# Attention and a routed feed-forward layer on one core: four payload buffers, the last group's scatters set among the tiles, and the words of all tiles loaded from SyncE's queue

## What is computed

```python
x = x + xattn(ctx, ctx, layernorm(x), Wk, Wv, bv, Wq, bq, Wo, bo)
xt = layernorm(x).reshape(-1, D)                       # 4096 tokens
p = softmax(xt @ Wr + br); probs, idx = top_k(p, 2); probs /= probs.sum()
h = layernorm(relu(xt @ W1[e] + b1[e])) * g1[e] + be1[e]
y = layernorm(relu(h @ W2[e] + b2[e])) * g2[e] + be2[e]
x = x + sum over the token's two experts of gate * y
```

## Time and profile before

| what | value |
| --- | --- |
| time, median of 3 runs | 272.37 us (269.18 to 274.11) |
| profiled execution, from first to last instruction | 268.4 us |
| between the two, taken as what lies around the span | 4.0 us |
| TensorE busy | 239.9 us (89%) |
| VectorE busy | 229.7 us (86%) |
| ScalarE busy | 211.5 us (79%) |
| GpSimd busy | 190.6 us (71%) |
| mean granted TensorE clock | 0.955 |

### The profile page before, as it was taken

How to read it: one execution, slowest core, us unless ns; L and a number is a source line. 1 busy time by engine, 2 the same in 40 slices (tenths; PEclk the granted TensorE clock), 3 DMA queues, 4 the chain that set the end, 5 groups by cost and what they waited for, 6 DMA issues and landing times.

```text
span 268.4 us, 10286 instructions
## 1 busy us (share of the span) xinstructions
PE 239.9 (89%) x2960; PEld 194.0 (72%) x2960; DVE 229.7 (86%) x1091; ACT 211.5 (79%) x795; POOL 190.6 (71%) x300
## 2 busy tenths in 40 slices
PE   1989779899888677679899999999999999999994
PEld 1564567777666434579899979999999999999330
DVE  0667986867689989689999988999999999999875
ACT  2465675789888888757999988999999999999700
POOL 8602277877757777775888888888888888878640
PEclk9997995899999759999999999999999999999999
DMA  6998398123425234354333443333315686772257
GB/s 159 313 299 295 91 271 279 51 89 92 139 82 136 83 91 99 84 119 94 84 90 67 89 82 81 73 72 75 84 33 142 155 155 141 149 143 86 68 187 233
DMA packets 48676, 34.56 MB, mean 129 GB/s; under 512 B 26871, under 2 KB 42743, under 8 KB 48620
## 3 DMA queue, kind: packets, MB, share of 16 engines
q1 hardware_dynamic: 38972, 22.80, 32.8%
q0 software_dynamic: 6592, 9.00, 12.7%
q10 hardware_dynamic: 3056, 2.11, 2.6%
HBM read 15.11 MB, written 12.02 MB: 101 GB/s over the span
## 4 chain that ended last, share of the span: by engine, by line
DVE 37%; issue 22%; PE 20%; ACT 9%; DMA 5%; DVEq 4%; SPq 1%; ACTq 0%
PE bank L721 15%; DVE vo L1873 8%; PE bank L725 4%; DMA w2f<-in_L_ffn_W 3%; DVE rs L1914 3%; DVE cx L1903 3%; DVE kq L1866 3%; DVE w2f L1653 3%; DVEq L1880 2%; DVE st L1891 2%; ACT ex L1175 2%; DVE mv L1897 1%; DMA wr<-in_L_ffn_Wr 1%; ACT xt L1198 1%; DVE topi L1573 1%
## 5 line engine op out<-in xcount | busy, mean ns | idle before, releaser
L679 POOL DMA_INDIRECT answers<-vo,words_of x71 | 70.6, 994 | 23.8 <-issue 19.4
L667 POOL DMA_INDIRECT slot_rows<-pay,pos x64 | 65.5, 1023 | 27.9 <-issue 18.5
L721 PE MATMUL bank<-kb_room,w1h 128*128 128x128 f16 x568 | 55.2, 219 | 1.7 <-issue 1.7
L725 PE MATMUL bank<-w2h,rh 128*128 x284 | 51.4, 219 | 1.6 <-ACT w2l L1122 1.6
L725 PE MATMUL bank<-rh 128*128 128x129 f16 x284 | 51.5, 220 | 0.0
L725 PE MATMUL bank<-w2l,rh 128*128 x284 | 51.4, 219 | 0.0
L721 PE MATMUL bank<-kb_room,w1l 128*128 128x128 f16 x284 | 51.2, 219 | 0.0
L1866 DVE SCALAR_TENSOR_TENSOR kq<-bank,rh 128x512 f16<-128x512 f32 x71 | 47.8, 673 | 0.1
L721 PEld LDWEIGHTS bank<-kb_room,w1h 128*128 x568 | 43.6, 98 | 2.6 <-issue 2.6
L1347 ACT ACTIVATE rh<-bank 128x512 f16<-128x512 f32 x71 | 41.1, 579 | 5.2 <-PE bank L721 4.2
L705 POOL DMA_DIRECT2D words_of<-slot_rows x71 | 40.8, 576 | 2.0 <-issue 1.8
(11 more groups left out here) (259 smaller groups left out, 601.7 us busy)
## 6 DMA issues: line engine op xcount, KB each, us to landing
x_tok<-in_x SPq DMA_DIRECT2D x8, 256.0 KB, 7.7
w1f<-in_L_ffn_W SPq DMA_DIRECT2D x2, 1024.0 KB, 8.8
pay<-pay SPq DMA_DIRECT2D x8, 256.0 KB, 3.3
w1f<-answers SPq DMA_DIRECT2D x8, 256.0 KB
w2f<-answers SPq DMA_DIRECT2D x8, 256.0 KB, 2.9
kb_room<-slot_rows SPq DMA_TRANSPOSE x71, 3.3
words_of<-slot_rows POOLq DMA_DIRECT2D x71, 1.0 KB
answers<-vo,words_of POOLq DMA_INDIRECT x71
```

The source lines that it names most:

```text
L667: eng.indirect_dma_start(slot_words, bass.IndirectOffsetOnAxis(ap=pos[:, g % 2, k, i:i + 1], axis=0), pay[g % 2][:, k, i, :].bitcast(U32), ...
L679: eng.indirect_dma_start(answers, bass.IndirectOffsetOnAxis(ap=words_of[:, j % NW, 0:1], axis=0), z[j % NZ], None).then_inc(s_ans[j % NZ], 16)
L721: return eng.matmul(dst, lhsT, rhs, start=start, stop=stop)
L725: return eng.matmul(dst, lhsT, rhs, start=start, stop=False, skip_group_check=True)
```

## The change

- `pay`, `pos` and the semaphores `s_copy` and `s_sc` are four (NP = 4) where they were two; group g waits for the scatters of group g - 4.
- All 8 scatters of the last group are issued among the tiles, at p = 0, 2, ..., 14.
- `words` moves from GpSimd to SyncE. `words(j)` is issued right behind the transposing load of tile j + 8 (`WORDS_BEHIND`), and the last eight behind the last tile's load. It takes the row number from the register that the load of tile j used. It waits for the answers of tile j - 12 and for `gate_share(j - 8)`.
- GpSimd has neither the word loads nor the register loads for them.
- Smaller edits free room and semaphores: `b2row` and `w2_rows` lie in rows of `w2_mean` and `c2`, the load of `b2row` goes ahead of W1's, several semaphores are joined, and some waits are merged with their neighbours.

```diff
+    NP = 4
-        b2row = sb("b2row", [1, E * D])
-        w2_rows = sb("w2_rows", [2, E * D])
         c2 = sb("c2", [P, E * D])
+        b2row, w2_rows = w2_mean[0:1, :], c2[0:2, :]
-        pay = [sb(f"pay{n}", [P, K, GT, ROW], F16) for n in range(2)]
+        pay = [sb(f"pay{n}", [P, K, GT, ROW], F16) for n in range(NP)]
-        NW, NS, LEAD = 12, 8, 2
+        NW, NS = 12, 8
+        WORDS_BEHIND = E
@@ sync
+            def words(j):
+
+                if j >= NW:
+                    eng.wait_ge(s_ans[(j - NW) % NZ], answered(j - NW))
+                if j >= NS:
+                    eng.wait_ge(s_rg, j - NS + 1)
+                eng.dma_start(words_of[:, j % NW, :], slot_words[bass.ds(place_of[j], P), D:]).then_inc(s_word[j % NS], 16)
...
                     for j in range(NX):
                         tile_rows(j)
+                        if j >= WORDS_BEHIND:
+                            words(j - WORDS_BEHIND)
...
                 tile_rows(j)
+                words(j - WORDS_BEHIND)
 
                 if j in back_at:
                     answers_back(back_at[j])
 
+            for j in range(SLOT_TILES - WORDS_BEHIND, SLOT_TILES):
+                words(j)
@@ gpsimd
-            for g in range(GROUPS):
+            for g in range(GROUPS - 1):
                 for k in range(K):
                     for i in range(GT):
-                        if g < GROUPS - 1 or k == 0:
-                            payload_out(g, k, i)
+                        payload_out(g, k, i)
+            last_out = [(GROUPS - 1, k, i) for k in range(K) for i in range(GT)]
...
-            for j in range(LEAD):
-                words(j)
             for p in range(SLOT_TILES + 4):
                 if 0 <= p - 4 < SLOT_TILES:
                     answer(p - 4)
-                if p + LEAD < SLOT_TILES:
-                    words(p + LEAD)
-
-                if p % 3 == 2 and p // 3 < GT:
-                    payload_out(GROUPS - 1, 1, p // 3)
+                if p % 2 == 0 and p // 2 < K * GT:
+                    payload_out(*last_out[p // 2])
@@ scalar (and likewise in pos_ and gate_rows)
-                if g >= 2:
-                    eng.wait_ge(s_sc[g % 2], scattered(g - 2))
+                if g >= NP:
+                    eng.wait_ge(s_sc[g % NP], scattered(g - NP))
```

More of the change, by code:

```diff
@@ L388, in build @@
                 "rstd2_guess", "xt", "pay_hi", "pay_lo", "mask", "pe_rank", "pos", "pe_base"))
-        s_copy = [signal(f"pay_copy{n}") for n in range(2)]
-        s_sc = [signal(f"scatter{n}") for n in range(2)]
+        s_copy = [signal(f"pay_copy{n}") for n in range(NP)]
+        s_sc = [signal(f"scatter{n}") for n in range(NP)]
         q_stat, q_root1, q_root2, q_max, q_sum, q_top, q_pos, q_scale, q_tab, q_gate = (signal(n) for n in (
@@ L395, in build @@
         s_diff, s_gexp, s_gated, s_gate = (signal(n) for n in ("gate_diff", "gate_exp", "gates_in_rows", "gates"))
[L397 to L402, removed]
+        s_share, p_share, s_shareT, p_off = (signal(n) for n in (
+            "shares", "pe_shares", "sharesT", "pe_offsets"))
+        s_gm, s_ss, p_tot, s_tot, s_scale, s_w1x = (signal(n) for n in (
+            "gains", "square_sums", "pe_totals", "totals", "scale", "w1_less_last"))
         p_rows, s_rows_, st_sums, ld_off, s_c2, p_low, s_low = (signal(n) for n in (
@@ L428, in scattered, with rows_out @@
         def scattered(n):
-            return 16 * K * GT * (n // 2 + 1)
+            return 16 * K * GT * (n // NP + 1)
+        def rows_out(eng, groups):
+            for g in range(max(groups - NP, 0), groups):
+                eng.wait_ge(s_sc[g % NP], scattered(g))
         def answered(j):
@@ L483, in sync @@
             eng.dma_start(gb[NB:2 * NB, :], flat("L0_ffn_be1").rearrange("(c p) -> c p", p=P)).then_inc(ld_gb, 16)
+            eng.dma_start(b2row[:, :], flat("L0_ffn_b2").rearrange("(o n) -> o n", o=1)).then_inc(ld_gb, 16)
             for h in range(2):
@@ L489, in sync @@
                                   ).then_inc(ld_w1[h], 16)
-            eng.dma_start(b2row[:, :], flat("L0_ffn_b2").rearrange("(o n) -> o n", o=1)).then_inc(ld_b2, 16)
-            eng.wait_ge(s_diag, 1)
+            eng.wait_ge(s_zeros, 1)
             for n in range(2):
@@ L510, in sync @@
             regs = [eng.alloc_register(f"row{n}") for n in range(2 * E)]
-            rows = []
+            place_of = {}
             def tile_rows(j):
@@ L518, in tile_rows @@
                     table = row_tab[:, 0:WHOLE] if j < WHOLE else row_tab[:, :]
-                    rows[:] = rows_of(half_regs, table, j, 0, E * REGION + (SPARE - 1) * P)
-                here = bass.ds(rows[j % E], P)
-                eng.dma_start_transpose(xsT[j % NX], slots[here, 0:2 * D]).then_inc(s_row[j % NX], 16)
+                    rows = rows_of(half_regs, table, j, 0, E * REGION + (SPARE - 1) * P)
+                    place_of.update({j + n: row for n, row in enumerate(rows)})
+                eng.dma_start_transpose(xsT[j % NX], slots[bass.ds(place_of[j], P), 0:2 * D]).then_inc(s_row[j % NX], 16)
+            def words(j):
[4 more added lines that the diff above has]
+                eng.dma_start(words_of[:, j % NW, :], slot_words[bass.ds(place_of[j], P), D:]).then_inc(s_word[j % NS], 16)
             for g in range(GROUPS):
@@ L527, in sync @@
                     eng.wait_ge(s_tab, 1)
[L528 to L529 removed]
+                    rows_out(eng, AHEAD)
                     for j in range(NX):
                         tile_rows(j)
+                        if j >= WORDS_BEHIND:
+                            words(j - WORDS_BEHIND)
                 eng.wait_ge(s_lo, g + 1)
[L533 removed]
+                eng.dma_start(pay[g % NP][:, 1, :, 0:2 * D], pay[g % NP][:, 0, :, 0:2 * D]).then_inc(s_copy[g % NP], 16)
                 if g in (3, 4):
@@ L573, in sync @@
                     eng.wait_ge(s_zero, 16 * (E + 1))
-                    for n in range(2):
-                        eng.wait_ge(s_sc[n], scattered(GROUPS - 2 + n))
+                    rows_out(eng, GROUPS)
                     eng.wait_ge(s_tab, 2)
                 tile_rows(j)
+                words(j - WORDS_BEHIND)
                 if j in back_at:
                     answers_back(back_at[j])
+            for j in range(SLOT_TILES - WORDS_BEHIND, SLOT_TILES):
+                words(j)
             for g in range(GROUPS - 2, GROUPS):
@@ L601, in gpsimd @@
                 eng.memset(second[:, n:n + 1], float(n))
-            eng.memset(be2_diag[:, :], 0.0).then_inc(s_diag, 1)
+            eng.memset(be2_diag[:, :], 0.0)
             eng.memset(zero_rows[:, :, :], 0.0).then_inc(s_zeros, 1)
-            for n in range(2):
+            for n in range(NP):
                 eng.memset(pay[n][:, 0, :, D - 1:D], 1.0)
@@ L681, in answer @@
                     z[j % NZ], None).then_inc(s_ans[j % NZ], 16)
[L683 to L699, removed]
-                    n = min(E, table.shape[1] - j)
-                    eng.load(half_regs[0:n], table[:, j:j + n])
-                    rows[:] = [eng.snap(r, min_val=0, max_val=E * REGION + (SPARE - 1) * P) for r in half_regs[0:n]]
-                if j >= NW:
-                    eng.wait_ge(s_ans[(j - NW) % NZ], answered(j - NW))
-                eng.dma_start(words_of[:, j % NW, :], slot_words[bass.ds(rows[j % E], P), D:]).then_inc(s_word[j % NS], 16)
-            for j in range(LEAD):
-                words(j)
             for p in range(SLOT_TILES + 4):
@@ L1743, in gate_rows @@
                 tiles = slice(g * GT, (g + 1) * GT)
-                to = [pay[g % 2][:, k, :, 2 * D + 2:2 * D + 4].bitcast(F32)[:, :, 0] for k in range(K)]
+                to = [pay[g % NP][:, k, :, 2 * D + 2:2 * D + 4].bitcast(F32)[:, :, 0] for k in range(K)]
                 if k == 0:
```

59 lines of the change are left out of this document (28 added, 31 removed).

## The result

| | before | changed |
| --- | --- | --- |
| time, median of 4 runs each, in turn on one chip | 273.24 us (269.18 to 275.53) | 298.21 us (296.7 to 299.3) |
| span of the profiled execution | 268.4 us | 296.5 us |
| mean granted TensorE clock | 0.955 | 0.956 |

The ratio is 1.100, with a 95% interval from 1.090 to 1.110. The change makes the kernel slower by a tenth. The clock is the same, so the 28.1 us of span are waiting and not slower work.

What follows compares the result with a forecast made beforehand. VectorE and TensorE set the 1.86 us step; SyncE's overfull queue starts tile 70's load 17.4 us after the latest harmless start, 237.3. Span 268.4 + 17.4 - 0.9 = 284.9, plus 4.0 is 288.9 us; 8-in-10 range 278 to 300.

Steps and rivals of the forecast that it cites:

- Rival 1: SyncE's queue: its room of 15.5 us hides word loads cheaper than 0.25 us each; 271.5 us, chance 0.10.
- Rival 3: Tile steps: GpSimd is the bound, so without words the step falls to 1.83 us; 269.4 us, chance 0.03.
- rival 4: TensorE in the tile stage: the clock falls because it now idles each step; well over 300 us, chance 0.02.
- rival 2: SyncE's queue: word loads behind transposing loads cost 0.82 us, 306.8 us (296.3 at 0.65); chance 0.15 for over 300.
- I take 0.53: SyncE's queue: price in us of one word load, from the zero-row loads, with 0.42 and 0.82 as bounds.
- The term that was left as it is: SyncE's long issues, transposing loads up to 2.50 us instead of 1.17: kept within the 122.2 us, no separate size.
- Where it melts: Tile stage: SyncE's 2.25 us per tile against a 1.86 us step uses up its lead in the first part.
- Four buffers, 0: GpSimd's payload buffers: the wait for scatters two groups back never bites, so removing it gains 0 us.
- Last scatters: Last group's scatters among the tiles: the last moves from 140.9 to about 146, SyncE arrives later itself; 0 us.
- Tail, -0.9 us: End of the kernel: GpSimd without words issues the last answers at 256.04 instead of 256.96, gaining 0.9 us.
- 4.0 us around the span: Whole kernel: the median of the runs lies 4.0 us over the profiled span, added to the forecast span.
- The rule on issuing engines: DMA starts gathered on SyncE: by the rule next to no cost, 271.5 us; the prediction said the trace disagrees.

Runs made afterwards that it cites:

- e1: Changed kernel with the words of all tiles issued by GpSimd again, four buffers and late scatters kept: 272.78 us, 1.005 of the kernel before.
- e8: Changed kernel with the words of tile j behind the load of tile j + 4 instead of j + 8, chip like the first: 298.5 us, 1.093.
- e7: The changed kernel run once more, unaltered, as reference on a chip like the first: 301.51 us, 1.104 of the kernel before.
- e2: Kernel before with only the words moved to SyncE, two buffers and old scatters kept: 302.23 us, ratio 1.110.
- e9: Changed kernel without the wait for `gate_share` in SyncE's word loads (12 semaphores for the words), chip like the first: 298.89 us, 1.095.
- e5: Changed kernel with words four tiles behind the rows instead of eight, on a slower chip: 342.95 us, where the kernel before took 330.02.
- e6: Changed kernel with 12 word semaphores instead of 8, so no wait for `gate_share`, on a slower chip: 342.77 us, where the kernel before took 330.02.
- e11: Every fourth tile's words on SyncE, the others on GpSimd, scatters where they were before the change, another slower chip: 327.65 us, 1.008 of the kernel before.
- e12: All words issued by ScalarE's queue at the end of each step, scatters where they were before the change, another slower chip: 338.02 us, 1.041.

## Why the prediction was right, and where it was wrong

The forecast was 288.9 us, with a range of its own from 282 to 296; measured are 298.2. The direction and the mechanism were right, the size was not.

**Direction and mechanism.** That VectorE and TensorE hold the step, and that SyncE has too little room: as forecast. The marks that it named are there: the waits of 14.3 us nearly gone, GpSimd waiting in nearly each step (65 of 71), VectorE and TensorE idle. But they are idle for 26 to 28 us rather than 17, and the last transposing load is at 265.3 and not between 250 and 257. Rival 1 (SyncE has room) falls with the table: one word load would have had to cost 0.25 us, and costs 0.65 to 0.78. Rival 3 falls with GpSimd's 97.6 us of waits and an unchanged time of the others, and rival 4 with a granted clock of 1.00 from 180 to 200 us, in spite of TensorE's pauses in each step. What came is the middle of rival 2 (dearer loads: 296.3 us at 0.65, 306.8 at 0.82).

**The step that failed: "I take 0.53".** In its own sum, the queue occupied for 122.2 us and the last load 62 word loads later, one of them costs 0.72 us in the changed kernel, not 0.53. Redone with what was measured:

| term | predicted | measured |
| --- | --- | --- |
| first transposing load | 99.6 | 98.1 |
| occupied without words | 122.2 | 122.2 (e1: 123.1) |
| 62 word loads | 32.9 (0.53 each) | 44.5 (0.72 each) |
| waits left | 0 | 0.5 |
| start of tile 70's load | 254.7 | 265.3 |
| late against 237.3 | 17.4 | 28.0 |
| tail | -0.9 | 0 |
| span, 268.4 + late + tail | 284.9 | 296.4 (profile: 296.5) |

Down to the start of tile 70's load the right column agrees by construction, since 0.72 was worked out from it. The test of the sum is the rest: a load 28.0 us late makes the span 28.1 us longer. The 4.3 us from the start of that load to ScalarE's use of words 62 were 4.5 (265.26 to 269.78). The load came 10.6 us later than forecast: 11.6 from the price and 0.5 of waits, less 1.5 for the earlier start.

The 0.53 came from eight zero-row loads in a row, and was chosen for its form (128 rows at an address from a register). In the undisturbed period above 1.93 us go from one transposing load to the next with a word load between them. With nothing between them and no wait, in the kernel before, it is (3.80 - 1.17) / 2 = 1.31 us (the 1.93 of the earlier trace rows hold waits for TensorE):

```profile
202.27 3.80 SPq L521 DMA_TRANSPOSE kb_room<-slot_rows  x3
```

So a word load adds 0.62 us, 0.37 for the issue and 0.25 around it, where 0.33 and 0.20 were taken. The remaining 0.10 of 0.72 are the long issues of the next paragraph and what else differs between the two executions. The row that stands behind a transposing load gave 0.65 and was in the bounds. It was the nearer one, in part by luck: its issue of 0.45 was too long and its 0.20 for the rest too short. How much of the 0.62 comes from the neighbour is seen behind the last transposing load of e8, where five word loads stand in a row:

```profile
270.65 2.67 SPq L536 DMA_DIRECT2D words_of<-slot_rows  x5
```

The first four starts are (2.67 - 0.33) / 4 = 0.58 us apart, with 0.33 for an issue. So about half of the 0.09 between 0.53 and 0.62 comes with this kind of load (its two waits may be the reason; nothing was run to tell), and about half is that the issue takes 0.37 behind a transposing load.

**The term that was left as it is.** "If the word loads have them too it is worse": they have. Twelve of 71 took 0.65 us or more, and the 71 issues sum to 35.2 us where 71 x 0.37 is 26.3. The transposing loads kept long ones of their own, up to 2.03 us, but over 1.17 they have 7.3 us in all where it was 11.2 before. How much falls on the word loads changes from execution to execution: the 62 ahead of tile 70's load have 8.5 us over 0.37 each here, 4.2 in e7 and 3.2 in e2. The long ones often lie where instructions are fetched: 20 of the changed kernel's 24 (transposing loads over 1.30 us, word loads over 0.60) begin within 0.6 us of one of the 25 fetches of 16 KB, or one starts while they last. Before there were such pairs too, as a fetch at 138.4 us and a load of 2.27 us at 137.9. Nothing was run to test that, so it stays a coincidence in time.

**Where it melts.** Forecast was that the lead goes in the first part and SyncE then sets the step. It does: the delay of ScalarE's first relu of a tile, against before, is -0.3 us at tile 12, 3.9 at tile 17, 10.7 at tile 44 and 28.1 at tile 70. The queue's work for a tile was forecast at 2.25 us and is 166.7 / 71 = 2.35.

**Four buffers, 0.** As forecast as far as the runs reach: the first write of each group's buffer comes 1.3 to 1.5 us earlier from the start on, group 1's as much as group 7's, so nothing was gained from group to group. e1 has them and is not faster.

**Last scatters, "so 0".** Right in the changed kernel, wrong as a rule. The last scatter is at 146.0 as forecast (about 146), and SyncE does not wait for it, since it arrives late itself. But with the words on GpSimd this placement makes a wait of 11.0 us where the forecast for such a queue was 3. The likely reason: it counted three steps of the answers' delay, and not that GpSimd, with eight scatters among its tiles rather than four, and a step of 1.86 us without them, falls behind in the stretch itself.

**Tail, -0.9 us.** ScalarE's last rows, and GpSimd's last answers:

```profile
282.77 0.40 ACT L1376 ACTIVATE vo<-cx,rg 128x128 f32<-128x128 f32 x1
```

```profile
282.89 0.96 POOL L697 DMA_INDIRECT answers<-vo,words_of  x1 [0.30 <-ACT vo L1376]
284.15 1.19 POOL L697 DMA_INDIRECT answers<-vo,words_of  x1 [0.30 <-issue]
```

The rows are ready at 283.17 and the answers go out at 284.15, 0.98 us behind. Before it was 256.96 - 255.08 = 1.88. So the 0.9 are there, and do not reach the end: from the last rows to the end of the span it is 13.3 us in both. From `gate_share` of tile 62 to the end it is 26.8 us before and 26.7 in the changed kernel, e2, e7 and e9, so this term is 0 in all four. The last group's load and its store came 7.15 us apart (286.73 and 293.88) where it had been 5.2 (260.56 and 265.77). Why that took longer was not tried.

**4.0 us around the span.** The profiled execution of the changed kernel took 298.25 us with a span of 296.5, so only 1.75 us lie around it. In every other run on record a time is 1.6 to 1.9 us over its span as well. So the span of 268.4 us belongs to an execution of about 270 us, a fast one, and not to the median of 272.37. This error made the miss smaller, which is luck: 288.9 + 10.6 of the queue + 0.9 of the tail - 2.3 here is 298.1.

**The rule on issuing engines.** The Trainium skill (DMA: Bandwidth & Descriptors, section Issuing engines are not separate DMA queues) calls the sequencer's time to start a DMA usually small relative to the DMA. The trace does not agree here: a transposing load's issue is 1.17 us beside 3.2 to its landing, a word load's 0.37 beside 1.8. With the register work around them they fill 1.93 us where the step was 1.86, and to move 71 starts of a DMA from GpSimd to SyncE cost 10%.

## What to carry to other kernels

An engine that issues nothing but DMAs shows no busy row, so count it out before giving it more: first to last issue, less its waits, is what it is occupied for, and its waits are all the room there is. Price a DMA that goes into such a queue by a row that stands behind the same neighbour as it will, and not by one of the same shape in a run of its kind alone: its waits, its neighbour and the long issues each add a little. On this queue that row's 0.53 stood against 0.65 for the row behind the same neighbour, with 0.62 in an undisturbed period and 0.68 to 0.72 on average in the kernels with all words on SyncE. Work taken from an engine that nobody waits for buys nothing, and a wait that such an engine makes for another (11.0 us at tile 24) can use up the room that the next edit counts on.

## What was not expected of the hardware

- The price of starting a load of 128 rows of 8 bytes between transposing loads: 0.62 us in an undisturbed stretch, 0.65 to 0.78 on average, on SyncE. The DMA issue itself took 0.37 us there, 0.34 on ScalarE's queue, and 0.58 on GpSimd's before the change (0.57 in the earlier trace rows).
- e5 and e6 ran on one chip, e11 and e12 on another, on which the kernel before took 330 and 326 us instead of 272. From 20 to 100 us of the span, in the routing, the granted clock was 0.87 on the first chip (changed kernel) and 0.72 on the last (e12). The rows of that stretch, the changed kernel and then e12:

```profile
20.00:100.00 80.00, 67.92 (x550) 48.85 (x549) 66.17 (x408) 62.08 (x185) 54.01 (x63) 0.87 0.47 144
```

```profile
20.00:100.00 80.00, 63.77 (x422) 47.50 (x422) 48.12 (x291) 44.06 (x139) 37.84 (x47) 0.72 0.37 118
```

- On the chip of e5 and e6, kernels with all words on SyncE were 4 to 5% slower than before and not 10. There the queue is not full from end to end: in e5 SyncE waited 13.2 us for `gate_share` before its word loads, in e6 11.1 us at tile 24. What costs the 4% there stays open. Ratios from chips of different pace should not be put into one table, and here they are not.
